# A macaron layer on one core: the second mixture of experts starts one attention step earlier

## The chip, the cores and the metric

The kernel runs on 1 core of one Trainium2 chip. The metric is the device time of one execution in microseconds (us); of several executions the median counts. TensorE multiplies matrices into the eight PSUM banks, VectorE (DVE), ScalarE (ACT) and GpSimd (POOL) do the rest, SyncE (SP) issues transfers. Each engine works through its own row of instructions in order and waits on semaphores for the others.

## The reference, cut to what matters

```python
x = x + 0.5 * ffn(layernorm(x), Wg, We, be)      # first MoE
x = x + attn(layernorm(x), Wq, Wk, Wv, Wo, Wf)   # attention
x = x + 0.5 * ffn(layernorm(x), Wg, We, be)      # second MoE
```

x is 16 sequences x 256 tokens x 128. `ffn` takes the softmax of x @ Wg over 8 experts, keeps the best 2, weighs them to a sum of 1, and adds gate * (x @ We[e] + be[e]). `attn` has 16 heads of 8; the scores of query i and key j are q.k * scale + c_i - c_j, with c the cumulative sum of log_sigmoid(x @ Wf), causal, then softmax, times v, times Wo.

## The kernel before

All of x stays in SBUF (`x_all`, 32 tiles of 128 tokens). **The MoE** goes through 8 groups of 4 tiles; its step s has four parts (`part(i, s, q)`, q = 0 to 3) on each engine and does three things for three groups at once. For group s + 2 (flag N): statistics (VectorE, line 339), rstd and shift on POOL (lines 226 to 233, part 0), xn on ScalarE (line 275, part 1), its transposes on TensorE (line 458, part 3), and their split in two parts (ScalarE line 267, VectorE line 391, part 3). For group s + 1 (flag A): twelve small matmuls to the logits (lines 447 to 449, part 1), then the gate chain on VectorE (lines 357 to 401, parts 1 to 3). For group s (flag B): per part one tile, with six matmuls of 512 columns into a low and a high bank (lines 416 and 417), four weighted sums of the low half on VectorE (line 294), four scalings of the high half on ScalarE (line 251), their sums on POOL (`add_upper`, lines 217 and 221); in part 0 also the transposed gates (lines 434, 264) and the bias (lines 441, 344). So steps -2 and -1 only prepare, and steps 0 to 7 use the experts.

**Attention** is a pipeline over sequences. Its step i has six parts: the scores of sequence i without transposition and their row maxima (lines 881 to 889; VectorE line 794), a split of the maxima on POOL (`split_max`, lines 684, 686, parts 2 and 5), their transposes (line 930) and a transfer into an extra row of q; for sequence i - 1 the turned scores (line 901), exponentials (ScalarE line 733), a causal mask per part (POOL line 673) and the product with v (line 916); for sequence i - 2 the end of it: transposes, normalisation (lines 822, 824), output projection (lines 991, 997), addition to x (line 871). The projections run two sequences ahead. Step 14 is full but for projections; step 15 has the last scores; step 16 has only turned scores (sequence 15) and the end of sequence 14; step 17 only the end of sequence 15.

The order is written out by hand in `run_layers`: `beside` takes a string in which each "a" is the next part of an attention step and each "m" the next part of an MoE step, and every engine follows that string in its own row.

The eight banks are shared. Attention uses banks 0 and 1 for scores, 2 and 3 for turned scores, 4 and 5 for the output, 6 for small things, 7 for projections (`proj_bank`, the q/k bank). The second MoE takes banks 1 and 3 as low, 2 and 4 as high, 0 for logits and transposed gates, 7 for transposes and bias. Its first tile waits until the attention's banks are free (`attn_done`, `wt_exp`).

Of the kernel before, what the change touches and what calls it, by code (L numbers as in the profile page):

```python
# [4 lines left out]
FP32 = mybir.dt.float32  # L5
# [4 lines left out]
ACT = mybir.ActivationFunctionType  # L10
AX = mybir.AxisListType

P = 128
# [4 lines left out]
def at_least(eng, sem, value):  # L18

    if isinstance(value, int) and value <= 0:  # L20
        return
    eng.wait_ge(sem, value)
# [8 lines left out]
def run_steps(eng, step, first, last, body, unroll, after=None):  # L31

    lo, hi = body
    for i in range(first, lo):
        step(i, i)
        if after is not None:
            after(i)
    with eng.Fori(0, (hi - lo) // unroll) as k:  # L40
        for part in range(unroll):
            step(k * unroll + (lo + part), lo + part)
    for i in range(hi, last):
        step(i, i)


def run_layers(eng, moe1, attention, moe2, groups, seqs, after=None):


    def moe_steps(part, first, last, after=None):  # L50
        run_steps(eng, lambda i, s: [part(i, s, k) for k in range(4)], first, last, (2, groups - 2), 2, after)

    def beside(order, i_attention, moe, i_moe):

        for at, which in enumerate(order):
            done = order[:at].count(which)
            if which == "a":
                attention(i_attention, i_attention, done)
            else:
                moe(i_moe, i_moe, done)  # L60

    moe_steps(moe1, -2, groups - 2, after)
    beside("amamammaaa", -2, moe1, groups - 2)
    beside("amamammaaa", -1, moe1, groups - 1)
    run_steps(eng, lambda i, s: [attention(i, s, k) for k in range(6)], 0, seqs - 1, (2, 2 + (seqs - 5) // 3 * 3), 3)
    beside("amaamamaam", seqs - 1, moe2, -2)
    beside("amaamamaam", seqs, moe2, -1)
    beside("aaaamamamm", seqs + 1, moe2, 0)
    moe_steps(moe2, 1, groups)


# [94 lines left out]
def moe_layer(nc, ctx, c, made, tiles, banks, x_all, tag, x_dram=None, out_dram=None, before=None):  # L166
# [5 lines left out]
    E, Q, G = c["E"], 4, x_all.shape[1] // 4  # L172
# [6 lines left out]
    y_low = [banks[0], banks[2]]  # L179
    y_high = [banks[1], banks[3]]  # L180
    gate_bank = banks[4]
    gates_t_view = gate_bank[0:3 * Q * E, P:2 * P]
    xt_bank = bias_bank = banks[5]
    logits = gate_bank[:, 0:Q * E].rearrange("p (q e) -> p q e", e=E)

    x_in = sem("x_in")
    stat_done, mom_done, eps_done = sem("stat_done"), sem("mom_done"), sem("eps_done")
# [1 line left out]
    xt_ready, hi_ready, lo_ready = sem("xt_ready"), sem("hi_ready"), sem("lo_ready")  # L189
    logits_ready, chain = sem("logits_ready"), sem("gate_chain")  # L190
    no_ready, egap_ready = sem("no_ready"), sem("egap_ready")
# [53 lines left out]
    def scalar(act):  # L245
        def experts(i, s, q):
            t = i * Q + q
            act.wait_ge(y_ready, t + 1)
            at_least(act, pair_done, t - 1)
            for j in range(4):  # L250
                last = nc.scalar.activation(scaled[:, q % 2, j], y_high[q % 2][:, j * D:(j + 1) * D], ACT.Copy,  # L251
                                            scale=gates[:, s % 2, q, 4 + j:5 + j])
            last.then_inc(high_used, 1)

        def exp_gap(i):
            act.wait_ge(chain, (i + 1) * CH + 2)
            nc.scalar.activation(egap[:, :], gap[:, :], ACT.Exp).then_inc(egap_ready, 1)

        def part(i, s, q):
            b, n = s % 2, i + 3  # L260
            N, A, B = s + 2 < G, -1 <= s and s + 1 < G, 0 <= s
            if q == 0 and B:
                act.wait_ge(gates_t_ready, i + 1)
                nc.scalar.activation(gates_t[:, :], gates_t_view, ACT.Copy).then_inc(gates_t_copied, 1)
            if q == 3 and N:
                act.wait_ge(xt_ready, n)
                nc.scalar.activation(xt_hi[:, b], xt_bank[:, :], ACT.Copy).then_inc(hi_ready, 1)
            if B:
                experts(i, s, q)
            if q == 1 and A and s >= 0:  # L270
                exp_gap(i)
            if q == 1 and N:
                act.wait_ge(shift_done, n)
                for k in range(Q):
                    last = nc.scalar.activation(xn[:, k], x_all[:, bass.ds((i + 2) * Q + k, 1), :].rearrange("p a d -> p (a d)"),  # L275
                                                ACT.Identity, scale=rstd[:, b, k:k + 1], bias=shift[:, b, k:k + 1])
                last.then_inc(xn_done, 1)
            if q == 1 and A and s < 0:
                exp_gap(i)
        return part  # L280

    def vector(dve):
# [39 lines left out]
        def part(i, s, q):  # L322
            N, A, B = s + 2 < G, -1 <= s and s + 1 < G, 0 <= s
            a, b, m, n = (s + 1) % 2, s % 2, i + 3, i + 2
            flat = gates[:, a].rearrange("p q e -> p (q e)")
            early = x_dram is not None and s < 0

            if early and s == -2 and q == 0:
# [78 lines left out]
    def tensor(pe):  # L407
        def experts(i, s, q):
            t = i * Q + q
            b = s % 2  # L410
            at_least(pe, low_chain, (t - 1) * 4)
            at_least(pe, high_used, t - 1)
            hi, lo = xt_hi[:, b, q * P:(q + 1) * P], xt_lo[:, b, q * P:(q + 1) * P]
            H = 4 * D
            for k, (x_part, w_part) in enumerate(((hi, c["we_hi"]), (hi, c["we_lo"]), (lo, c["we_hi"]))):
                nc.tensor.matmul(y_low[q % 2][:, :], x_part, w_part[:, 0:H], start=k == 0, stop=k == 2)  # L416
                last = nc.tensor.matmul(y_high[q % 2][:, :], x_part, w_part[:, H:2 * H], start=k == 0, stop=k == 2)  # L417
            last.then_inc(y_ready, 1)

        def part(i, s, q):  # L420
            a, n = (s + 1) % 2, i + 2
            N, A, B = s + 2 < G, -1 <= s and s + 1 < G, 0 <= s
            if s == -1 and q == 0 and x_dram is not None:
                pe.wait_ge(made["weights_split"], 1)
            if s == -2 and q == 3 and x_dram is not None:
                pe.wait_ge(made["filled"], 2)
            if s == 0 and q == 0 and x_dram is None:
                pe.wait_ge(before["attn_done"], 4 * G - 1)
                pe.wait_ge(before["wt_exp"], 2 * G * 12)
            if B:  # L430
                experts(i, s, q)
            if q == 0 and B:
                pe.wait_ge(gates_ready, i + 1)
                nc.tensor.transpose(gates_t_view, gates3[:, :, :].rearrange("p k n -> p (k n)").bitcast(FP32),
                                    c["ident"][:, :]).then_inc(gates_t_ready, 1)
                pe.wait_ge(gates_t_copied, i + 1)
                if A:
                    pe.wait_ge(lo_ready, n)
                if s == 0 and x_dram is not None:
                    pe.wait_ge(made["bias_hi"], 2)  # L440
                nc.tensor.matmul(bias_bank[:, :], gates_t[:, :], c["bias_split"][:, :],
                                 start=True, stop=True).then_inc(bias_ready, 1)
            if q == 1 and A:
                pe.wait_ge(lo_ready, n)
                for k in range(Q):
                    hi, lo = xt_hi[:, a, k * P:(k + 1) * P], xt_lo[:, a, k * P:(k + 1) * P]
                    nc.tensor.matmul(logits[:, k], hi, c["wg_hi"][:, :], start=True, stop=False)
                    nc.tensor.matmul(logits[:, k], hi, c["wg_lo"][:, :], start=False, stop=False)
                    last = nc.tensor.matmul(logits[:, k], lo, c["wg_hi"][:, :], start=False, stop=True)
                last.then_inc(logits_ready, 1)  # L450
            if q == 3 and N:
                pe.wait_ge(xn_done, i + 3)
                if B:
                    pe.wait_ge(bias_added, i + 1)
                else:
                    at_least(pe, lo_ready, n)
                for k in range(Q):
                    last = nc.tensor.transpose(xt_bank[:, k * P:(k + 1) * P], xn[:, k], c["ident"][:, :])
                last.then_inc(xt_ready, 1)
        return part  # L460
# [5 lines left out]
def attention_layer(nc, ctx, c, made, banks, x_all, S_LEN, before):  # L466
# [407 lines left out]
    def tensor(pe):  # L874
# [58 lines left out]
        def part(i, s, j):  # L933
# [75 lines left out]
            if j == f_part(s) + 1 and F:  # L1009
# [5 lines left out]
    return dict(constant_rows=constant_rows, sync=sync, set_up_rows=set_up_rows, zero_rows=zero_rows, set_up_zero=set_up_zero, set_up_dense=set_up_dense,  # L1015
                set_up_columns=set_up_columns, set_up_masks=set_up_masks,
                order_columns=order_columns, gpsimd=gpsimd, scalar=scalar, vector=vector, tensor=tensor,
                x_done=proj_added, attn_done=attn_done, wt_exp=wt_exp)


def program(nc, x, Wq, Wk, Wv, Wo, Wf, Wg, We, be, out):
    B, N, D = x.shape
    H, E = Wf.shape[1], Wg.shape[1]
# [3 lines left out]
    with ExitStack() as ctx:  # L1027
# [17 lines left out]
        tiles = moe_tiles(nc, ctx, E, Q, D)  # L1045
        moe1 = moe_layer(nc, ctx, c, made, tiles, banks, x_all, "m1_", x_dram=x_rows)
        attention = attention_layer(nc, ctx, c, made, banks, x_all, N, before=moe1)
        moe2 = moe_layer(nc, ctx, c, made, tiles, banks[1:5] + [banks[0], banks[7]], x_all, "m2_",
                         out_dram=out_rows, before=attention)
        block = ctx.enter_context(nc.Block())  # L1050

# [70 lines left out]
```

## Time and profile before

| what | value |
|---|---|
| three runs | 469.98, 466.66, 469.72 us; median 469.72 |
| profiled execution | 468.03 us, of which 465.9 us span (first to last instruction) |
| busy share of the span | TensorE 87%, VectorE 78%, ScalarE 60%, POOL 54% |
| mean granted TensorE clock | 0.978 of full |
| row maximum, line 794 | 192 times, mean 685 ns |
| exponential, line 733 | 192 times, mean 591 ns |
| DMA | 84 GB/s mean; nearly none from step 15 on |

The profiled execution is one run; the 2.1 us beside its span are launch and end. A stage is a stretch of the span that I cut at the first matmul of an attention step. Busy time is not needed time: what matters in a stage is which wait ends last. A wait in the trace names the instruction that waited, and behind the arrow the one that released it.

### The profile page before, as it was taken

What the parts mean: (1) busy time and instruction counts of PE and PEld (TensorE: products, weight loads), DVE (VectorE), ACT (ScalarE), POOL (GpSimd) and SP (SyncE); (2) the same over time, 40 slices, a digit from 0 to 9 for tenths busy, and PEclk for the clock granted to TensorE, in tenths of its full rate; (3) what the DMA queues carried; (4) which work ended last, traced back from release to release, by engine and by line L of the source; (5) the groups of instructions that cost most, each with busy time, mean ns of one, the idle gap of its engine ahead of it and who ended that gap; (6) DMA issues with size and microseconds to landing.
All of it is one profiled execution on the core that took longest, in us unless ns stands there. A gap on an engine that the chain in (4) does not pass through costs nothing.

```text
span 465.9 us, 11688 instructions
## 1 busy us (share of the span) xinstructions
PE 404.1 (87%) x3280; PEld 287.6 (62%) x3296; DVE 362.4 (78%) x1284; ACT 278.5 (60%) x758; POOL 249.7 (54%) x431
## 2 busy tenths in 40 slices
PE   0778888775799999999999999999998898888884
PEld 0656666553466666666667666766765676666652
DVE  3989999986877786686677678677666458999995
ACT  4666777352275566657566566655656567667753
POOL 8976666543245544544554454454445435676654
PEclk9999999887999999999999999999999899999998
DMA  3311000035644354344535535443540000001001
GB/s 112 92 56 22 0 1 0 1 100 148 171 118 152 117 155 116 111 139 111 149 102 147 134 102 149 113 147 108 152 130 9 6 1 1 25 24 45 23 23 45
DMA packets 45792, 39.11 MB, mean 84 GB/s; under 512 B 5896, under 2 KB 42524, under 8 KB 45754
## 3 DMA queue, kind: packets, MB, share of 16 engines
q1 hardware_dynamic: 43706, 38.14, 29.0%
q10 hardware_dynamic: 2048, 0.53, 0.6%
q8 instruction: 17, 0.28, 0.3%
q14 instruction: 21, 0.17, 0.1%
HBM read 22.61 MB, written 15.20 MB: 81 GB/s over the span
## 4 chain that ended last, share of the span: by engine, by line
PE 43%; POOL 22%; issue 14%; ACT 8%; DVE 5%; DMA 2%; ACTq 2%; SPq 2%; POOLq 1%; DVEq 0%
PE bank L916 10%; POOL m_pair L217 9%; PE bank L901 8%; PE bank L886 6%; ACT a_weights L733 5%; POOL m_upper L221 4%; PE bank L889 4%; PE bank L881 4%; POOL m_rstd L229 3%; PE bank L997 2%; PE bank L1008 2%; ACTq L725 2%; PE bank L1011 2%; DVE a_neg_max L794 1%; DMA x_all<-in_L_attn_x 1%
## 5 line engine op out<-in xcount | busy, mean ns | idle before, releaser
L794 DVE TENSOR_REDUCE a_neg_max<-bank 128x2 f32<-128x512 f32 (+1 forms) x192 | 123.7, 685 | 62.6 <-PE bank L889 59.9
L673 POOL TENSOR_SCALAR_AFFINE_SELECT a_weights<-a_weights 128x512 f32<-128x512 f32 (+1 forms) x96 | 75.5, 787 | 108.7 <-ACT a_weights L733 104.0
L733 ACT ACTIVATE a_weights<-bank 128x512 f32<-128x512 f32 x192 | 107.0, 591 | 35.0 <-issue 22.0
L251 ACT ACTIVATE m_scaled<-bank,m_gates 128x128 f32<-128x128 f32 x256 | 72.3, 365 | 26.2 <-PE bank L417 26.2
L901 PE MATMUL bank<-a_q_rows,a_k_rows 106*128 106x512 f32 (+1 forms) x192 | 73.7, 451 | 4.9 <-ACT a_weights L733 4.9
L217 POOL TENSOR_TENSOR m_pair<-m_scaled 128x256 f32<-128x256 f32 x64 | 47.5, 742 | 50.8 <-ACT m_scaled L251 50.7
L294 DVE SCALAR_TENSOR_TENSOR m_lower<-bank,m_gates,m_lower 128x128 f32<-128x128 f32 x192 | 66.0, 344 | 2.3 <-issue 0.2
L886 PE MATMUL bank<-a_k_rows,a_q_rows 104*128 104x256 f32 x256 | 59.3, 335 | 0.4 <-DVE a_neg_max L794 0.4
L889 PE MATMUL bank<-a_mask,a_ident 128*128 128x256 bf16 (+1 forms) x176 | 56.2, 320 | 0.0
L916 PE MATMUL bank<-a_weights,a_v 128*32 128x128 f32 x1536 | 52.7, 279 | 0.0
L886 PEld LDWEIGHTS bank<-a_k_rows,a_q_rows 104*128 104x128 f32 x256 | 40.6, 194 | 14.5 <-DVE a_neg_max L794 10.1
L916 PEld LDWEIGHTS bank<-a_weights,a_v 128*32 128x32 f32 x1536 | 39.6, 111 | 8.9 <-issue 6.4
L416 PE MATMUL bank<-we_hi,m_xt_hi 128*128 128x512 f32 x64 | 32.1, 502 | 11.9 <-DVE m_lower L294 11.3
L901 PEld LDWEIGHTS bank<-a_q_rows,a_k_rows 106*128 106x128 f32 (+1 forms) x192 | 30.9, 193 | 13.4 <-ACT a_weights L733 11.4
L881 PE MATMUL bank<-a_k_heads,a_q_dense 104*128 104x512 f32 x64 | 31.1, 524 | 5.9 <-DMA a_k_heads<-k_stage 4.4
L720 ACT ACTIVATE a_max_t<-bank 32x128 fp32r<-32x128 f32 x32 | 8.5, 265 | 42.3 <-PE bank L930 42.3
L221 POOL TENSOR_TENSOR m_upper<-m_pair 128x128 f32<-128x128 f32 x64 | 29.6, 463 | 5.7 <-POOL m_pair L217 1.3
L889 PEld LDWEIGHTS bank<-a_mask,a_ident 128*128 128x128 bf16 x192 | 19.0, 99 | 19.4 <-issue 12.5
L275 ACT ACTIVATE m_xn<-x_all,m_shift,m_rstd 128x128 f32<-128x128 f32 (+1 forms) x64 | 26.3, 484 | 4.6 <-POOL m_shift L233 4.5
L416 PEld LDWEIGHTS bank<-we_hi,m_xt_hi 128*128 128x128 f32 x64 | 12.5, 196 | 22.6 <-DVE m_lower L294 22.1
L417 PE MATMUL bank<-we_hi,m_xt_hi 128*128 128x512 f32 x64 | 26.2, 409 | 0.0
L417 PE MATMUL bank<-we_lo,m_xt_hi 128*128 128x512 f32 x64 | 26.2, 409 | 0.0
(128 smaller groups left out, 828.5 us busy)
## 6 DMA issues: line engine op xcount, KB each, us to landing
a_k_rows<-k_stage SPq DMA_DIRECT2D x16, 416.0 KB
k_stage<-a_k_parts SPq DMA_DIRECT2D x48, 128.0 KB, 1.8
q_stage<-a_q_parts SPq DMA_DIRECT2D x48, 128.0 KB, 1.9
a_q_rows<-q_stage SPq DMA_DIRECT2D x64, 96.0 KB
a_k_heads<-k_stage SPq DMA_DIRECT2D x64, 52.0 KB
a_q_dense<-q_stage SPq DMA_DIRECT2D x16, 192.0 KB
x_all<-in_L_attn_x SPq DMA_DIRECT2D x8, 256.0 KB, 2.8
out_x<-x_all SPq DMA_DIRECT2D x8, 256.0 KB, 2.3
```

Source lines behind the costliest of these rows:

```text
L217: nc.gpsimd.tensor_tensor(pair[:, q % 2], scaled[:, q % 2, 0:2], scaled[:, q % 2, 2:4], ALU.add).then_inc(pair_done, 1)
L251: last = nc.scalar.activation(scaled[:, q % 2, j], y_high[q % 2][:, j * D:(j + 1) * D], ACT.Copy, scale=gates[:, s % 2, q, 4 + j:5 + j])
L294: nc.vector.scalar_tensor_tensor(out=lower[:, q % 2, j], in0=y_low[q % 2][:, j * D:(j + 1) * D], scalar=gates[:, s % 2, q, j:j + 1], in1=t ...
L417: last = nc.tensor.matmul(y_high[q % 2][:, :], x_part, w_part[:, H:2 * H], start=k == 0, stop=k == 2)
L673: nc.gpsimd.affine_select(out=diagonal, in_=diagonal, compare_op=ALU.is_ge, fill=0.0, base=0, pattern=[[0, heads.stop - heads.start], [1, P]],
L733: nc.scalar.activation(weights[n // 2][:, half:half + 4, :].rearrange("p h n -> p (h n)"), wt_bank[n % 2][:, :], ACT.Exp).then_inc(wt_exp, 1)
L794: nc.vector.tensor_reduce(neg_max[:, t, heads], score_bank[p % 2][:, :].rearrange("p (h n) -> p h n", n=(t + 1) * P), AX.X, ALU.max, negat ...
L881: nc.tensor.matmul(bank[:, :], q_dense[:, p, :], k_heads[:, p:H:NU, :], start=True, stop=False, skip_group_check=True)
L886: nc.tensor.matmul(bank[:, n * keys:(n + 1) * keys], q_rows[b][0:KR, h, P:N], k_rows[b][0:KR, h % NU, :], start=n == 0, stop=False, skip_g ...
L889: nc.tensor.matmul(own, ident16[:, :], mask16[:, 0:heads, :], start=False, stop=True, skip_group_check=True).then_inc(scores_ready, 1)
L901: nc.tensor.matmul(bank[:, :], k_rows[b][0:rows, u, jt * P:(jt + 1) * P], q_rows[b][0:rows, u:H:NU, t * P:(t + 1) * P], start=True, stop=T ...
L916: last = nc.tensor.matmul(out_bank[t][32 * g:32 * (g + 1), u // 2 * P:(u // 2 + 1) * P], v_sb[b][:, jt * H // 2 + 2 * g + u // 2, u % 2:u ...
```

## The change

The MoE steps -2 and -1 of the second MoE move from attention steps 15 and 16 to 14 and 15. Of step 0, part 0 (tile 0) moves into step 16, behind the fifth attention part; parts 1 to 3 stay in step 17. The second MoE's banks become 0 and 2 low, 1 and 3 high, 4 for logits and gates. Since bank 4 is still the attention's in step 15 and 16, the logits and transposed gates of group 0 go to bank 7; that adds the waits for `no_ready` and `lo_ready`. Tile 0 uses banks 0 and 1 and waits for the last row maximum (`max_done`) alone; the two old waits move to tile 1.

```diff
-    run_steps(eng, lambda i, s: [attention(i, s, k) for k in range(6)], 0, seqs - 1, (2, 2 + (seqs - 5) // 3 * 3), 3)
-    beside("amaamamaam", seqs - 1, moe2, -2)
-    beside("amaamamaam", seqs, moe2, -1)
-    beside("aaaamamamm", seqs + 1, moe2, 0)
+    run_steps(eng, lambda i, s: [attention(i, s, k) for k in range(6)], 0, seqs - 2, (2, 2 + (seqs - 5) // 3 * 3), 3)
+    beside("amaamamaam", seqs - 2, moe2, -2)
+    beside("amaamamaam", seqs - 1, moe2, -1)
+    beside("aaaaama", seqs, moe2, 0)
+    beside("aaamamama", seqs + 1, moe2, 0, 1)
...
-    gates_t_view = gate_bank[0:3 * Q * E, P:2 * P]
-    logits = gate_bank[:, 0:Q * E].rearrange("p (q e) -> p q e", e=E)
+    bank_ahead = lambda g: xt_bank if g == 0 and x_dram is None else gate_bank
+    gates_t_view = lambda g: bank_ahead(g)[0:3 * Q * E, P:2 * P]
+    logits_view = lambda g: bank_ahead(g)[:, 0:Q * E].rearrange("p (q e) -> p q e", e=E)
...
             if s == 0 and q == 0 and x_dram is None:
+                pe.wait_ge(before["max_done"], 2 * G * 12)
+            if s == 0 and q == 1 and x_dram is None:
                 pe.wait_ge(before["attn_done"], 4 * G - 1)
                 pe.wait_ge(before["wt_exp"], 2 * G * 12)
...
                 pe.wait_ge(gates_ready, i + 1)
-                nc.tensor.transpose(gates_t_view, gates3[:, :, :].rearrange("p k n -> p (k n)").bitcast(FP32),
+                if s == 0 and x_dram is None:
+                    pe.wait_ge(lo_ready, n)
+                nc.tensor.transpose(gates_t_view(s), gates3[:, :, :].rearrange("p k n -> p (k n)").bitcast(FP32),
...
                     at_least(pe, lo_ready, n)
+                    if s == -1 and x_dram is None:
+                        pe.wait_ge(no_ready, n)
...
-        moe2 = moe_layer(nc, ctx, c, made, tiles, banks[1:5] + [banks[0], banks[7]], x_all, "m2_",
+        moe2 = moe_layer(nc, ctx, c, made, tiles, banks[0:5] + [banks[7]], x_all, "m2_",
```

The added lines shift the numbers: in the changed kernel line 673 is 683, 217 is 219, 221 is 223, 226 to 233 are 228 to 235, 901 is 911, 916 is 926, 416 and 417 are 419 and 420, 794 is 804, 391 is 394.

POOL's row in step 16 and at the head of step 17, before; each AFFINE_SELECT is a causal mask of sequence 15, and the last of them stands at the end of the x4:

```order
L673 AFFINE_SELECT a_weights<-a_weights 128x1024
L226 TENSOR_SCALAR m_var_eps<-m_moments 128x4
L227 TENSOR_SCALAR m_neg_mean<-m_moments 128x4
L229 TENSOR_TENSOR m_rstd<-m_var_eps,minus_half 128x4
L233 TENSOR_TENSOR m_shift<-m_neg_mean,m_rstd 128x4
L673 AFFINE_SELECT a_weights<-a_weights 128x1024
L673 AFFINE_SELECT a_weights<-a_weights 128x512 x4
L217 TENSOR_TENSOR m_pair<-m_scaled 128x256
L221 TENSOR_TENSOR m_upper<-m_pair 128x128
```

The same place in the changed kernel:

```order
L683 AFFINE_SELECT a_weights<-a_weights 128x1024 x2
L683 AFFINE_SELECT a_weights<-a_weights 128x512 x3
L219 TENSOR_TENSOR m_pair<-m_scaled 128x256
L223 TENSOR_TENSOR m_upper<-m_pair 128x128
L228 TENSOR_SCALAR m_var_eps<-m_moments 128x4
L229 TENSOR_SCALAR m_neg_mean<-m_moments 128x4
L231 TENSOR_TENSOR m_rstd<-m_var_eps,minus_half 128x4
L235 TENSOR_TENSOR m_shift<-m_neg_mean,m_rstd 128x4
L683 AFFINE_SELECT a_weights<-a_weights 128x512
```

The rstd group left the head of the step, and the last mask now stands behind the upper sum of tile 0 and the rstd group of group 2.

TensorE's row at the end of step 16 and the head of step 17, before; turned scores 8 to 11 are the two x2 of line 901, and line 916 the products with v:

```order
L901 MATMUL bank<-a_q_rows,a_k_rows 128x512 x2
L991 MATMUL bank<-ident,a_attn 128x128 x2
L901 MATMUL bank<-a_q_rows,a_k_rows 128x512 x2
L925 MATMUL bank<-ident,a_out_t 128x128 x2
L997 MATMUL bank<-wo,a_attn_t 128x128 x2
L916 MATMUL bank<-a_weights,a_v 32x128 x16
L458 MATMUL bank<-ident,m_xn 128x128 x4
L916 MATMUL bank<-a_weights,a_v 32x128 x16
L925 MATMUL bank<-ident,a_out_t 128x128 x2
L416 MATMUL bank<-we_hi,m_xt_hi 128x512
```

In the changed kernel, from tile 0 to the products with v:

```order
L419 MATMUL bank<-we_hi,m_xt_hi 128x512
L420 MATMUL bank<-we_hi,m_xt_hi 128x512
L419 MATMUL bank<-we_lo,m_xt_hi 128x512
L420 MATMUL bank<-we_lo,m_xt_hi 128x512
L419 MATMUL bank<-we_hi,m_xt_lo 128x512
L420 MATMUL bank<-we_hi,m_xt_lo 128x512
L442 MATMUL bank<-ident,m_gates 96x128
L449 MATMUL bank<-bias_split,m_gates_t 128x512
L911 MATMUL bank<-a_q_rows,a_k_rows 128x512 x2
L935 MATMUL bank<-ident,a_out_t 128x128 x2
L1007 MATMUL bank<-wo,a_attn_t 128x128 x2
L926 MATMUL bank<-a_weights,a_v 32x128 x32
```

Tile 0 with its gates and bias moved ahead of turned scores 10 and 11; the transposes of line 458 are gone from here, so that the products with v of steps 16 and 17 stand in one piece.

VectorE's row in step 15, before; each TENSOR_REDUCE is a row maximum:

```order
L794 TENSOR_REDUCE a_neg_max<-bank 128x4 x2
L339 BN_STATS m_stats<-x_all 128x6 x4
L348 BN_AGGR m_moments<-m_stats 128x2 x4
L794 TENSOR_REDUCE a_neg_max<-bank 128x4 x2
L794 TENSOR_REDUCE a_neg_max<-bank 128x2 x4
L822 RECIPROCAL a_recip<-bank 128x16
```

And in the changed kernel:

```order
L394 TENSOR_TENSOR m_xt_lo<-bank,m_xt_hi 128x512
L804 TENSOR_REDUCE a_neg_max<-bank 128x4 x2
L342 BN_STATS m_stats<-x_all 128x6 x4
L351 BN_AGGR m_moments<-m_stats 128x2 x4
L804 TENSOR_REDUCE a_neg_max<-bank 128x4 x2
L804 TENSOR_REDUCE a_neg_max<-bank 128x2 x2
L360 MAX m_best<-bank 128x8 x4
L380 TENSOR_TENSOR m_gap<-m_best 128x4
L382 MAX_INDEX m_best_no<-m_best,bank 128x8 x4
L804 TENSOR_REDUCE a_neg_max<-bank 128x2 x2
```

The low part of the transposes stands ahead of the first row maximum of the step, and the first piece of the gate chain between the sixth and the seventh.

## Rows read from the trace of the kernel before

**Rows 1.** Busy time by stage: stretch, its length, then busy us (instructions) of each engine, PEclk, DMA

```profile
337.65:351.67 14.02, 14.02 (x160) 9.94 (x157) 9.49 (x19) 8.41 (x18) 7.06 (x13) 1.00 0.43 116
351.67:366.63 14.96, 13.77 (x156) 9.45 (x153) 10.18 (x25) 9.33 (x21) 7.16 (x15) 1.00 0.02 4
366.63:381.18 14.55, 12.94 (x143) 9.03 (x139) 6.16 (x35) 9.47 (x22) 6.43 (x11) 0.88 0.01 3
381.18:395.54 14.36, 12.77 (x91) 9.42 (x90) 11.46 (x55) 8.89 (x30) 6.22 (x12) 1.00 0.00 1
```

**Rows 2.** Who waited for whom, step 15: total us, times, longest

```profile
PE bank L930 <- POOL a_max_parts L686: 0.8, 1, 0.8
```

**Rows 3.** Timeline of POOL: start, us, line, operation [idle before <-releaser]

```profile
343.82 0.22 POOL L686 TENSOR_TENSOR a_max_parts<-a_neg_max,a_max_parts 128x16 fp32r<-128x16 f32 x1
...
377.31 0.63 POOL L673 TENSOR_SCALAR_AFFINE_SELECT a_weights<-a_weights 128x512 f32<-128x512 f32 x1 [2.23 <-ACT a_weights L733]
...
386.12 0.74 POOL L217 TENSOR_TENSOR m_pair<-m_scaled 128x256 f32<-128x256 f32 x1 [5.45 <-ACT m_scaled L251]
...
386.94 0.46 POOL L221 TENSOR_TENSOR m_upper<-m_pair 128x128 f32<-128x128 f32 x1
...
389.18 0.20 POOL L233 TENSOR_TENSOR m_shift<-m_neg_mean,m_rstd 128x4 f32<-128x4 f32 x1
```

**Rows 4.** Timeline of TensorE, steps 14 to 17

```profile
345.06 0.27 PE L930 MATMUL bank<-ident,a_max_parts 128*32 128x128 f32 x1
...
353.29 0.40 PE L881 MATMUL bank<-a_k_heads,a_q_dense 104*128 104x512 f32 x1
...
366.63 0.66 PE L458 MATMUL bank<-ident,m_xn 128*128 128x128 f32 x4
...
370.51 1.94 PE L916 MATMUL bank<-a_weights,a_v 128*32 128x128 f32 x32
...
373.39 0.21 PE L447 MATMUL bank<-wg_hi,m_xt_hi 128*128 128x8 f32 x1
...
374.74 0.72 PE L901 MATMUL bank<-a_q_rows,a_k_rows 106*128 106x512 f32 x2
...
377.90 0.99 PE L901 MATMUL bank<-a_q_rows,a_k_rows 106*128 106x512 f32 x2
...
381.18 1.08 PE L916 MATMUL bank<-a_weights,a_v 128*32 128x128 f32 x32
...
382.96 0.48 PE L416 MATMUL bank<-we_hi,m_xt_hi 128*128 128x512 f32 x1
...
385.07 0.51 PE L441 MATMUL bank<-bias_split,m_gates_t 96*128 96x512 f32 x1 [0.36 <-ACT m_gates_t L264]
```

**Rows 5.** Timeline of ScalarE, steps 16 and 17

```profile
373.20 1.09 ACT L733 ACTIVATE a_weights<-bank 128x512 f32<-128x512 f32 x2 [1.99 <-PE bank L901]
...
374.44 1.65 ACT L275 ACTIVATE m_xn<-x_all,m_shift,m_rstd 128x128 f32<-128x128 f32 x4
...
384.92 1.12 ACT L251 ACTIVATE m_scaled<-bank,m_gates 128x128 f32<-128x128 f32 x4
```

**Rows 6.** Timeline of VectorE, steps 16, 17 and after

```profile
367.95 0.69 DVE L391 TENSOR_TENSOR m_xt_lo<-bank,m_xt_hi 128x512 fp32r<-128x512 f32 x1 [1.76 <-ACT m_xt_hi L267]
...
377.33 0.69 DVE L401 TENSOR_TENSOR m_hot<-m_hot,m_g 128x64 f32<-128x64 f32 x1
...
383.24 0.26 DVE L822 RECIPROCAL a_recip<-bank 128x16 f32<-128x16 f32 x1 [0.63 <-PE bank L925]
...
388.58 0.39 DVE L357 MAX8 m_best<-bank 128x8 f32<-128x8 f32 x4 [0.34 <-PE bank L449]
...
402.90 0.21 DVE L401 TENSOR_TENSOR m_hot<-m_hot,m_g 128x64 f32<-128x64 f32 x1
```

**Rows 7.** Busy time and granted clock of two stretches at the start of step 16

```profile
368.00:370.00 2.00, 0.56 (x2) 0.24 (x2) 1.80 (x9) 1.25 (x4) 0.00 (x0) 1.00 0.03 7
370.00:372.00 2.00, 2.00 (x29) 1.52 (x33) 0.00 (x0) 0.97 (x2) 1.78 (x4) 0.54 0.01 1
```

More of the change, by code:

```diff
@@ L51, in moe_steps, with beside @@
         run_steps(eng, lambda i, s: [part(i, s, k) for k in range(4)], first, last, (2, groups - 2), 2, after)
-    def beside(order, i_attention, moe, i_moe):
+    def beside(order, i_attention, moe, i_moe, first=0):
         for at, which in enumerate(order):
@@ L59, in beside @@
             else:
-                moe(i_moe, i_moe, done)
+                moe(i_moe, i_moe, first + done)
     moe_steps(moe1, -2, groups - 2, after)
@@ L263, in part @@
                 act.wait_ge(gates_t_ready, i + 1)
-                nc.scalar.activation(gates_t[:, :], gates_t_view, ACT.Copy).then_inc(gates_t_copied, 1)
+                nc.scalar.activation(gates_t[:, :], gates_t_view(s), ACT.Copy).then_inc(gates_t_copied, 1)
             if q == 3 and N:
@@ L325, in part @@
             flat = gates[:, a].rearrange("p q e -> p (q e)")
+            logits = logits_view(s + 1)
             early = x_dram is not None and s < 0
@@ L422, in part @@
             N, A, B = s + 2 < G, -1 <= s and s + 1 < G, 0 <= s
+            logits = logits_view(s + 1)
             if s == -1 and q == 0 and x_dram is not None:
@@ L1017, in attention_layer @@
                 order_columns=order_columns, gpsimd=gpsimd, scalar=scalar, vector=vector, tensor=tensor,
-                x_done=proj_added, attn_done=attn_done, wt_exp=wt_exp)
+                x_done=proj_added, attn_done=attn_done, wt_exp=wt_exp, max_done=max_done)
 def program(nc, x, Wq, Wk, Wv, Wo, Wf, Wg, We, be, out):
```

## The prediction

> **What bounds the kernel now.** I read first the busy time by stage [rows 1]. I call the 18 attention steps 0 to 17, as the code counts them. Step 14 is a full step (scores of sequence 14, turned scores of 13, projection of 12) with nothing of the second MoE beside it: TensorE is busy for all of its 14.02 us, VectorE for 9.49. Step 15 carries the first quarter-turn of the second MoE (its step -2) and takes 14.96 us, of which TensorE works 13.77. Step 16 has no scores any more, only turned ones, and MoE step -1 beside it: 14.55 us, with VectorE busy 6.16 and a mean granted clock of 0.88. Step 17 carries all four tiles of group 0: 14.36 us, VectorE 11.46. From 395.54 us on there is only MoE, in code that the change leaves as it is. So the change is worth what it does to the 57.89 us of these four stages; all their work stays, and only idle time can go or come. TensorE's idle time in them is 0 + 1.19 + 1.61 + 1.59 = 4.39 us, and some 1.4 us more lie in the slower clock of step 16. That, about 5.8 us, is the most that the change can gain.
>
> Next I read the waits of step 15 [rows 2]: TensorE stands once, for 0.8 us, at the transpose of the row maxima, because POOL splits them late, behind the four small operations of rstd. Then the timelines, one engine after the other [rows 3 to 6]. At the start of step 16 TensorE waits for exponentials: it does 0.56 us of work in 2 us, and in the next 2 us its granted clock is 0.54, so that it runs mostly at 1.2 GHz instead of 2.4 [rows 7]. The 32 matmuls of line 916 take 1.94 us there and 1.08 us in step 17 [rows 4].
>
> **Step 14 gets MoE step -2.** TensorE gains the four transposes of xn (0.6 us; they start at 366.63 and the next work at about 367.2 [rows 4]). They can't hide, since TensorE has no idle time here. POOL gains the rstd group ahead of its second causal mask. In step 17 that group runs from 387.40, where the upper sum ends, to 389.38: 2.0 us [rows 3]. In step 14 POOL finishes the first maxima at 344.04 without it [rows 3], and TensorE takes them at 345.06 [rows 4]. With it POOL ends at 346.05, so TensorE waits 1.0 us, much as the 0.8 us in step 15 shows [rows 2]. VectorE's statistics (1.3 us) fit in its 4.5 us of idle time, ScalarE's xn (1.65 us [rows 5]) in its 5.6. Step 14: +1.6 us. Bounds: +0.6 if POOL's group is hidden, +2.5 if ScalarE's xn adds another 0.9 to an exponential.
>
> **Step 15 gets step -1 in place of -2.** Statistics, rstd, xn and transposes it has already. New are: (a) xt_lo of group 0 at its head, which VectorE must do before the first row maximum. xt_lo ends 368.64 - 366.63 = 2.01 us after the transposes began [rows 4, 6]; a row maximum takes 0.69, so the first score bank comes free at 2.70. TensorE wants it 0.6 for the transposes + 1.62 (353.29 [rows 4] - 351.67 [rows 1]) = 2.22 us after that beginning. Cost 0.5, and 0.1 at the second bank. (b) The twelve logit matmuls, 374.74 - 373.39 = 1.35 us [rows 4]. They stand before the fourth part of the step, thus before the transpose that waited 0.8 us for POOL [rows 2], and take up that wait: cost 0.6. (c) VectorE's gate chain, some 3 us in three pieces: its work goes from 10.18 to about 13.2 + 0.7 = 13.9 us of a stage that grows to 16. The first piece (maxima, gap, indices, 1.2 us) runs while TensorE does two score groups, a transpose, two turned scores and line 916, some 3.5 us, against 1.2 + 2 x 0.69 = 2.6 us on VectorE. I cost it at nothing; if none of it were hidden it is the rival below. Step 15: +1.2 us (bounds 0.6 and 4.2).
>
> A row on the gate chain speaks against me: the product on line 401 took 0.69 us at 377.33, beside POOL's mask of 0.63 us from 377.31, and 0.21 us at 402.90 with POOL idle [rows 3, 6]. The Trainium skill, "SBUF — State Buffer", section "Who interferes with whom", says that a VectorE instruction with two inputs in SBUF and a GpSimd instruction that reads SBUF exclude each other for its whole length. The row agrees. Four more such operations of the chain now lie beside masks; by the rule each could lose up to the 0.5 us seen, 2 us in all, still inside VectorE's idle time; without the rule it is nothing.
>
> **Step 16 loses step -1 and gets tile 0.** I count in times of before, as if its head had not moved. The first 6.8 us stay, the waits and the slow clock too, as the same exponentials stand there. From 373.4 the logits go, but they stood in a wait: turned scores 6 need exponential 4, which ends at 373.75 [rows 5] against their start at 374.74 [rows 4], so 0.95 us are won. Then ScalarE's xn (1.65 us) no longer holds the exponentials back: line 916 ends at about 375.9, turned scores 8 and 9 and the transposes of the output at 376.65. Tile 0, the transposed gates and the bias take what they took in step 17, 382.96 to 385.42 = 2.45 us [rows 4]: 379.1. From turned scores 10 at 377.90 to 381.18 were 3.28 us [rows 4], less 0.6 for the transposes and 0.5 for a wait of these scores: 2.2. So step 17 begins at 381.3, where it began before, with tile 0 done.
>
> But the last causal mask is late. On POOL it now stands behind pair, upper sum and rstd of group 2. ScalarE scales tile 0 from 378.55 to 379.7 (1.12 us [rows 5]), pair and upper end 1.28 us later at 381.0, rstd (2.0) at 383.0, the mask (0.63) at 383.7 [rows 3]. TensorE has done the first half of line 916 at 381.8, waits 1.9 us, and ends the second at 384.2 (before: 382.26). Behind it in TensorE's row stand tile 1 and all of step 17.
>
> **Step 17 has three tiles.** Tile 1 takes 1.45 us (384.2 to 385.7), the logits 1.35: VectorE can start on them at 387.1, before at 388.58 [rows 6]: -1.5 us. Both kernels then have the same VectorE work, except that the normalisation of sequence 15 (two operations, the first 0.26 us [rows 6]; I take 0.5) now comes after that point and not before it. Steps 16 and 17: -1.0 us. The new waits cost nothing by themselves: lo_ready and no_ready are long past, max_done comes before step 16, and the attention waits of tile 1 are over at 382.5.
>
> **Sum.** +1.6 + 1.2 - 1.0 = +1.8 us. The profiled execution took 468.03 us (span 465.9, 2.1 around it), so it would be 469.8; on the median of 469.72 that is 471.5 us.
>
> **Rivals.** *The clock falls again* (0.22). A wait of 1.9 us is longer than the two of 0.7 and 0.8 that went ahead of the slow stretch of step 16. If it has the same effect, line 916, tile 1 and part of the logits run at 1.2 GHz: as much as before, 1.4 to 1.7 us. 471.5 + 1.6 = 473.1. Against it: TensorE was fully busy ahead of this wait.
>
> *VectorE becomes the bound of the full steps* (0.09). TensorE has two score banks and stands when VectorE is late with a maximum. If nothing of the added VectorE work hides, step 14 costs 1.9 and step 15 3.7 us (13.9 - 10.2) beside its 0.6 of TensorE: +6.2 - 1.0 = +5.2, 474.9 us, slower by 1.1%. It decides if the gaps of VectorE before its maxima in step 15 are gone. Against it: 4.5 us of idle time in step 14, and step 15 took 1.3 us of statistics without such a wait.
>
> *The mask is not late* (0.17). If POOL's queue runs ahead in step 14 and 17 (TensorE reaches both points later than I count), 1.0 and 1.9 us fall away: -1.1 us, 468.6. For it: the 0.8 us of rows 2 was all that POOL's order cost in step 15.
>
> *Most idle time goes* (0.04). The slow clock of step 16 stays away as well, and the waits at its head: near the most of 5.8 us; 464.5.
>
> My forecast has 0.48. The range of 8 in 10 goes from 467.5 to 475.2: the ends are the mask rival less 1 us and the VectorE rival. A difference of 1%, 4.7 us, is about what a measurement of this kernel can tell from none: faster by more 0.04, within it 0.86, slower by more 0.10.
>
> **What would show it.** Right: in the changed profile step 14 takes about 15.6 us and step 15 about 16.1; TensorE waits about 1 us at the transpose of the maxima in step 14 and no more in step 15; POOL's last causal mask comes 3 us after its last exponential and TensorE waits nearly 2 us for it; MoE step 1 begins about 1.8 us later than 395.54. Wrong: VectorE's maxima back to back through step 15 (second rival), a PEclk digit below full in step 17 (first), no wait of TensorE on POOL (third), or a step of the pure MoE tail that differs from before.

## The result, and the profile after

| | median | lowest | highest | executions |
|---|---|---|---|---|
| before | 466.75 us | 465.03 | 471.73 | 20 |
| changed | 470.18 us | 468.41 | 474.34 | 20 |

The ratio is 1.007 (95% interval 1.0046 to 1.0095): the change costs 3.3 us (2.1 to 4.4). The median of before is 3 us lower than the 469.72 us of the first three executions, from which the forecast was counted. The forecast was +1.8 us, with a rival of +3.4 us (the clock falls again). Ratios and means below leave out two executions in a slower state: one of the kernel before (471.27 us, clock 0.973) and one of g2_prep (627.13 us, clock 0.564).

The profiled execution of the changed kernel took 473.95 us, near the top of its range; its mean granted clock was 0.967. These are its busy times by stage, for step 14, step 15, and steps 16 and 17 together (from the transposes of line 468 to the first statistics of MoE step 1); columns as in [rows 1], where the last stage is 366.63 to 395.54:

```profile
337.33:352.72 15.39, 14.60 (x164) 10.41 (x161) 10.53 (x27) 9.72 (x22) 8.71 (x17) 1.00 0.42 105
352.72:368.96 16.24, 14.78 (x168) 10.82 (x166) 13.55 (x47) 10.04 (x23) 7.08 (x14) 1.00 0.02 4
368.96:399.02 30.06, 24.35 (x218) 17.55 (x215) 13.48 (x60) 16.58 (x47) 11.25 (x19) 0.89 0.01 2
```

Step 14 grew from 14.02 to 15.39 us, step 15 from 14.96 to 16.24, and the rest from 28.91 to 30.06. VectorE is busy for 13.55 us of step 15, as worked out (13.9); TensorE has 0.8 us of idle time in step 14, where it had none, and 1.5 in step 15.

TensorE's timeline of the same profile, at its waits. They stand where the forecast put them: 0.79 us for the split maxima in step 14 (line 940), 0.50 for the first row maximum of step 15 (line 891), 1.94 for the last causal mask (line 926). One of 0.96 us was priced at nothing (line 896, a row maximum behind the second piece of the gate chain). The transpose of the maxima in step 15, which waited 0.8 us before [rows 2], waits no more.

```profile
345.69 0.27 PE L940 MATMUL bank<-ident,a_max_parts 128*32 128x128 f32 x1 [0.79 <-POOL a_max_parts L696]
...
354.98 0.50 PE L891 MATMUL bank<-a_k_heads,a_q_dense 104*128 104x512 f32 x1 [0.50 <-DVE a_neg_max L804]
...
365.66 0.50 PE L896 MATMUL bank<-a_k_rows,a_q_rows 104*128 104x256 f32 x2 [0.96 <-DVE a_neg_max L804]
...
372.70 1.83 PE L926 MATMUL bank<-a_weights,a_v 128*32 128x128 f32 x32
...
377.58 1.94 PE L926 MATMUL bank<-a_weights,a_v 128*32 128x128 f32 x32
...
387.39 0.65 PE L926 MATMUL bank<-a_weights,a_v 128*32 128x128 f32 x16 [1.94 <-POOL a_weights L683]
```

And POOL at that last mask: pair and rstd of the MoE stand ahead of it, and TensorE goes on at 387.39, just after it ends at 387.25; the forecast's chain, link for link.

```profile
383.41 0.72 POOL L219 TENSOR_TENSOR m_pair<-m_scaled 128x256 f32<-128x256 f32 x1 [1.45 <-ACT m_scaled L253]
...
384.76 0.24 POOL L228 TENSOR_SCALAR m_var_eps<-m_moments 128x4 f32<-128x4 f32 x1
...
386.46 0.20 POOL L235 TENSOR_TENSOR m_shift<-m_neg_mean,m_rstd 128x4 f32<-128x4 f32 x1
...
386.61 0.64 POOL L683 TENSOR_SCALAR_AFFINE_SELECT a_weights<-a_weights 128x512 f32<-128x512 f32 x1
```

The second loss of this execution is the clock. After its head, step 16 ran slowly for about 7 us and not for 3.4 as in [rows 4, 7] (lines 926 at 1.83 and 1.94 us), and the clock fell once more in the plain MoE steps, from 403.6 to some 410. Two windows of the changed kernel; PEclk is the third number from the right:

```profile
375.00:378.00 3.00, 2.74 (x14) 1.37 (x16) 0.28 (x2) 2.45 (x5) 0.63 (x1) 0.50 0.02 5
405.00:408.00 3.00, 3.00 (x8) 2.31 (x9) 1.76 (x11) 1.35 (x5) 1.23 (x2) 0.50 0.00 0
```

So one profile against one profile says +6.0 us of span where the ratio says +3.3. A pair of executions that differ in their clock can't price a change; I needed more profiles.

### The profile page after: what moved, and what is told of

The parts are those of the page before. It is cut to its first block, busy times and chain, and to the rows that moved or that the text cites. A ratio compares the mean times of both kernels' runs of the same rounds, so it can differ in the third digit from the quotient of the medians.

```text
span 471.9 us, 11705 instructions
## 1 busy us (share of the span) xinstructions
PE 406.0 (86%) x3296; PEld 290.0 (61%) x3296; DVE 362.4 (77%) x1284; ACT 278.9 (59%) x758; POOL 249.4 (53%) x431
## 4 chain that ended last, share of the span: by engine, by line
PE 41%; POOL 19%; issue 13%; ACT 8%; DVE 8%; DMA 4%; SPq 4%; ACTq 2%; POOLq 1%; DVEq 0%
PE bank L926 9%; POOL m_pair L219 8%; PE bank L911 7%; PE bank L896 6%; ACT a_weights L743 5%; PE bank L899 4%; POOL m_upper L223 4%; PE bank L891 3%; POOL m_rstd L231 3%; PE bank L1007 2%; PE bank L1018 2%; PE bank L1021 2%; DVE m_lower L296 2%; ACTq L735 2%; DMA a_k_heads<-k_stage 1%
## 5 line engine op out<-in xcount | busy, mean ns | idle before, releaser
L899 PE MATMUL bank<-a_mask,a_ident 128*128 128x256 bf16 (+1 forms) x192 | 62.7, 327 | 0.0
L911 PEld LDWEIGHTS bank<-a_q_rows,a_k_rows 106*128 106x128 f32 (+1 forms) x192 | 31.3, 195 | 13.5 <-ACT a_weights L743 10.9
L296 DVE SCALAR_TENSOR_TENSOR m_lower<-bank,m_gates,x_all 128x128 f32<-128x128 f32 x64 | 21.7, 340 | 6.9 <-PE bank L420 6.1
```

What stands on the lines that cost most here:

```text
L296: nc.vector.scalar_tensor_tensor(out=lower[:, q % 2, j], in0=y_low[q % 2][:, j * D:(j + 1) * D], scalar=gates[:, s % 2, q, j:j + 1], in1=t ...
L899: nc.tensor.matmul(own, ident16[:, :], mask16[:, 0:heads, :], start=False, stop=True, skip_group_check=True).then_inc(scores_ready, 1)
L911: nc.tensor.matmul(bank[:, :], k_rows[b][0:rows, u, jt * P:(jt + 1) * P], q_rows[b][0:rows, u:H:NU, t * P:(t + 1) * P], start=True, stop=T ...
```

## The experiments

Each ratio is against the kernel before on the same chip. The runs e1 to e4 were on one chip, those with f and g on another, on which the changed kernel itself was not run.

| run | what | ratio | 95% interval |
|---|---|---|---|
| e4_same | changed kernel again | 1.0088 | 1.0054 to 1.0121 |
| e1_prep_only | no tile in step 16 | 1.0018 | 0.9985 to 1.005 |
| e2_mask_first / g3_mask | last mask first on POOL | 1.0029 / 0.9996 | 0.9999 to 1.0059 / 0.9964 to 1.0027 |
| e3_filled | waits filled with matmuls | 1.0069 | 1.0041 to 1.0096 |
| f2_dve | mask first, VectorE's order | 0.9994 | 0.9962 to 1.0027 |
| f3_all / g1_all | and POOL's, ScalarE's in step 14 | 0.9967 / 0.9945 | 0.9938 to 0.9996 / 0.9914 to 0.9976 |
| f4_prep_all / g2_prep | all orders, no tile in step 16 | 0.9984 / 0.9974 | 0.9952 to 1.0016 / 0.9943 to 1.0005 |

### Both kernels again

> The changed kernel once more, as a control on the same chip: ratio 1.005 to 1.0095 again. Its profile shows another execution: where the clock falls (step 16 for 3.4 or 6.8 us, and once in the MoE tail) differs from the first profile if that is chance; the waits of 0.8 us (step 14), 0.5 and 0.96 us (step 15) and 1.94 us (step 17) stand in it unchanged.

> The kernel before once more, for a second profile. Theory A: stages of 14.0 and 15.0 us for steps 14 and 15 again; step 16 and 17 together take 28.9 us if TensorE's clock falls in step 16 as in the first profile, and about 27.4 us if it doesn't, so that the change costs nothing or 0.2 us there instead of winning 1. Rival: steps 16 and 17 take 28.9 us with or without a fall of the clock.

In both new profiles the clock stays full through all four stages. Busy time by stage, the kernel before (466.19 us):

```profile
337.20:351.21 14.01, 14.01 (x160) 9.95 (x156) 9.50 (x19) 8.42 (x18) 7.05 (x13) 1.00 0.44 116
351.21:366.18 14.97, 13.78 (x156) 9.40 (x152) 10.11 (x25) 9.33 (x21) 7.04 (x15) 1.00 0.02 4
366.18:393.83 27.65, 24.19 (x233) 17.43 (x229) 17.25 (x89) 18.40 (x52) 12.67 (x23) 1.00 0.01 2
```

and the changed kernel:

```profile
337.02:352.42 15.40, 14.60 (x164) 10.37 (x161) 10.53 (x27) 9.73 (x22) 8.75 (x17) 1.00 0.41 105
352.42:368.67 16.25, 14.99 (x167) 10.81 (x165) 13.54 (x47) 10.04 (x23) 7.09 (x14) 1.00 0.02 4
368.67:396.30 27.63, 21.73 (x218) 15.74 (x215) 13.51 (x61) 16.48 (x47) 11.28 (x19) 1.00 0.01 2
```

Step 14 costs 1.39 us, step 15 1.28, steps 16 and 17 nothing (27.65 against 27.63): 2.65 us together. Without the fall of the clock the stage of before is 27.65 us and not 28.91, so the first profile held 1.3 us of slow clock there: theory A of f1_before (27.4) holds, its rival doesn't. The waits stand in the changed kernel's new profile too, with 0.80, 0.51 and 1.95 us; that of 0.96 was 0.75.

Turned scores 6 and 7 of step 16, which in the change lose the logits ahead of them, without a fall of the clock; first the kernel before, then the changed one:

```profile
372.78 0.71 PE L901 MATMUL bank<-a_q_rows,a_k_rows 106*128 106x512 f32 x2
```

```profile
374.62 0.98 PE L911 MATMUL bank<-a_q_rows,a_k_rows 106*128 106x512 f32 x2 [0.45 <-ACT a_weights L743]
```

They start 6.60 us after the stage's transposes before, and 5.95 after: 0.65 us are won here.

Part of the wait of 0.75 to 0.96 us in step 15 is the interference that the prediction had noted and taken to be hidden in VectorE's idle time. In the changed kernel's first profile, POOL's mask and the second piece of the gate chain ran side by side just before the maximum that TensorE wanted:

```profile
364.10 0.64 POOL L683 TENSOR_SCALAR_AFFINE_SELECT a_weights<-a_weights 128x512 f32<-128x512 f32 x1 [2.58 <-ACT a_weights L743]
```

```profile
364.24 0.50 DVE L399 TENSOR_TENSOR m_g<-m_egap,m_g 128x4 f32<-128x4 f32 x1
...
364.92 2.69 DVE L804 TENSOR_REDUCE a_neg_max<-bank 128x2 f32<-128x512 f32 x4
```

The mask and the product of line 399 both end at 364.74. In e4_same that product started ahead of the mask and took 0.16 us, and the next one (line 404) 0.59 instead of 0.22. So one of the two lost some 0.35 us in either profile.

The times agree. Every execution reports its mean granted clock. Of 90 executions of before (all those taken beside the runs of this section) 43 had 0.984 or more, mean 466.21 us; of 30 of the changed kernel 10, mean 468.91: +2.70 us (give or take 0.5) for the placement. Over all, the means are 467.37 and 470.53, +3.2 (give or take 0.8). The other 0.5 us is smaller than these uncertainties. It fits the clock: if a clock below 1 is taken as time at half speed, the changed kernel has 19.1 us of it per execution, before 16.8. That the change causes this isn't shown.

The end of step 17 shows a loss that I had priced too low. VectorE of the kernel before, from the logits (line 357) to the next step:

```profile
386.86 0.39 DVE L357 MAX8 m_best<-bank 128x8 f32<-128x8 f32 x4 [0.34 <-PE bank L449]
...
390.42 0.15 DVE L396 TENSOR_TENSOR m_g<-m_egap,m_g 128x4 f32<-128x4 f32 x1
...
390.75 0.50 DVE L401 TENSOR_TENSOR m_hot<-m_hot,m_g 128x64 f32<-128x64 f32 x1
...
393.10 0.55 DVE L303 TENSOR_TENSOR x_all<-m_lower,m_upper 128x128 f32<-128x128 f32 x1
...
393.83 0.86 DVE L339 BATCH_NORM_STATS2 m_stats<-x_all 128x6 f32<-128x128 f32 x4
```

and of the changed kernel (line 360 is 357 before, 399 is 396, 404 is 401, 305 is 303, 832 and 834 are 822 and 824):

```profile
388.26 0.39 DVE L360 MAX8 m_best<-bank 128x8 f32<-128x8 f32 x4 [0.99 <-PE bank L457]
...
390.17 0.24 DVE L832 RECIPROCAL a_recip<-bank 128x16 f32<-128x16 f32 x1
...
390.45 0.29 DVE L834 TENSOR_TENSOR a_attn<-bank,a_recip 128x128 f32<-128x128 f32 x1
...
391.96 0.70 DVE L399 TENSOR_TENSOR m_g<-m_egap,m_g 128x4 f32<-128x4 f32 x1
...
392.85 0.41 DVE L404 TENSOR_TENSOR m_hot<-m_hot,m_g 128x64 f32<-128x64 f32 x1
...
395.11 0.67 DVE L305 TENSOR_TENSOR x_all<-m_lower,m_upper 128x128 f32<-128x128 f32 x1
...
396.30 0.86 DVE L342 BATCH_NORM_STATS2 m_stats<-x_all 128x6 f32<-128x128 f32 x4
```

From the first of these rows to the last it takes 6.97 us before and 8.04 after. The normalisation at 390.17 is 0.5 of the difference, as forecast. Another 0.55 is the small product of line 399, 0.70 us where it was 0.15. POOL's pair sum ran just then:

```profile
391.84 0.80 POOL L219 TENSOR_TENSOR m_pair<-m_scaled 128x256 f32<-128x256 f32 x1 [2.42 <-ACT m_scaled L253]
```

It ends at 392.64 and the product at 392.66. That is the rule of the Trainium skill, "SBUF — State Buffer", section "Who interferes with whom": a VectorE instruction with two inputs in SBUF and a GpSimd instruction reading SBUF shut each other out. The measured 0.55 us agrees with it, and here VectorE had no idle time to hide it in. It isn't chance: this product took 0.69 or 0.70 us in the eight profiles with tile 0 in step 16 and 0.15 or 0.16 in the five without. No run moved the pair sum alone, so that the port is the cause rests on the page and on the two ends.

### No tile in step 16

```diff
-    beside("aaaaama", seqs, moe2, 0)
-    beside("aaamamama", seqs + 1, moe2, 0, 1)
+    beside("aaaaaa", seqs, moe2, 0)
+    beside("aaaamamamm", seqs + 1, moe2, 0)
```

> Only the two preparing MoE steps move to attention steps 14 and 15 (banks as in the changed kernel); step 16 has no MoE part, step 17 all four tiles. Theory A (costs by place: +2.6 us in steps 14 and 15, and the late last causal mask, 1.9 us, comes from tile 0 in step 16): steps 14 and 15 take 15.4 and 16.2 us as in the changed kernel, TensorE waits for no mask at the head of step 17, step 16 is about 2.4 us shorter than with tile 0, and the time is 0 to 1 us above the kernel before (ratio 1.000 to 1.002). Rival B (the slow clock does it: with the logits gone from step 16 TensorE idles more there, its clock stays low longer): the clock in step 16 is low for about 7 us instead of 3.4 in most profiles, and the time is as bad as the changed kernel's, ratio 1.005 or more.

TensorE has no wait for a mask at the head of step 17 here. Ratio 1.0018; steps 14 and 15 take 15.39 and 16.24 us as in the changed kernel. Steps 16 and 17, the clock full:

```profile
368.94:395.13 26.19, 22.34 (x217) 15.63 (x213) 13.05 (x60) 16.17 (x46) 11.03 (x19) 1.00 0.01 2
```

26.19 us against 27.63 with tile 0 in step 16. So as built, the tile in step 16, which has only turned scores, loses 1.4 us. Theory A's ratio and its steps 14 and 15 came out. Step 16 is 1.5 us shorter than with the tile and not 2.4, from the transposes to the products with v at its end (10.97 against 12.49). The clock rival is not borne out: with the logits gone from step 16 here as well, this profile shows no slow stretch there. But that is one profile, and the upper end of the interval is the rival's 1.005.

### The last mask first

The diff is cut: each engine also hands its name to `run_layers` as `who`.

```diff
-    beside("aaaaama", seqs, moe2, 0)
+    beside("aaaaaam" if who == "POOL" else "aaaaama", seqs, moe2, 0)
```

> The changed kernel with one change on POOL: in step 16 its MoE part comes behind the last causal mask. Theory A: TensorE's wait of 1.94 us for that mask goes, and nothing else is late, so 1.5 to 1.9 us less than the changed kernel, ratio to the kernel before 1.003. Rival B (clock): the ratio stays within 0.001 of the changed kernel's 1.007, as another part of step 17 waits instead or the clock eats it.

> e2_mask_first once more, to halve the uncertainty of what the late mask cost. Theory A: 2.2 us (27.63 - 25.44 between two undisturbed profiles) of the changed kernel's 3.3, ratio 1.002 to 1.004. Rival (the profile's 2.2 us come back elsewhere): 1.005 or more.

TensorE does all 64 matmuls with v in one piece, without a wait, and the stage takes 25.44 us:

```profile
380.26 1.96 PE L926 MATMUL bank<-a_weights,a_v 128*32 128x128 f32 x64
```

```profile
367.77:393.21 25.44, 21.50 (x218) 15.71 (x215) 13.47 (x60) 16.46 (x47) 11.28 (x19) 1.00 0.01 2
```

2.19 us less than with the mask behind the MoE part; g3_mask's profile has 25.43 us there. The ratios of the two runs, 1.0029 and 0.9996, lie about 2 and 3.5 us below the changed kernel's 1.007: more than half of the loss was this one place in POOL's queue. 0.9996 is lower than the 1.002 to 1.004 expected, though its interval reaches 1.0027. Tile 0 in step 16 then wins 0.75 us against e1 (25.44 against 26.19).

### Matmuls in the waits of step 16

```diff
+            if s == NSEQ - 1 and n in (2, 3):
+                if n == 2:
+                    pe.wait_ge(max_done, NSEQ * 12)
+                for _ in range(3):
+                    nc.tensor.matmul(score_bank[0][:, :], ident16[:, :], mask16[:, :, :], start=True, stop=True)
```

> The changed kernel with six matmuls of 512 columns into an unused score bank, in two lots of three, where TensorE waits for exponentials at the head of step 16 (they compute nothing that is used). Theory A (placement alone): each lot takes some 0.65 us inside a wait of 0.75 to 0.84, so the time stays, ratio 1.007. Rival B (clock): TensorE's clock no longer falls in step 16, 1.4 to 3.4 us less, ratio 1.001 to 1.004, and the granted clock of steps 16 and 17 is 1.00.

The waits of 0.74 and 0.84 us shrink to nothing and 0.18, at no cost (line 911 is now the added matmuls, 916 the turned scores; they start as long after the transposes as in e4_same, 1.97 and 3.31 us):

```profile
370.02 0.82 PE L911 MATMUL bank<-a_mask,a_ident 128*128 128x512 bf16 x3
...
370.93 0.50 PE L916 MATMUL bank<-a_q_rows,a_k_rows 109*128 109x512 f32 x1
...
371.27 0.82 PE L911 MATMUL bank<-a_mask,a_ident 128*128 128x512 bf16 x3
...
372.27 0.50 PE L916 MATMUL bank<-a_q_rows,a_k_rows 109*128 109x512 f32 x1 [0.18 <-ACT a_weights L743]
```

but the ratio is 1.0069, as without them. The clock stays full in step 16 of this profile and then falls at about 386, a microsecond after the wait of 1.95 us for the mask, for 10 us (0.58 is the mean of 12 us):

```profile
371.00:384.00 13.00, 10.97 (x143) 7.26 (x143) 4.38 (x18) 7.92 (x19) 6.78 (x11) 1.00 0.02 4
384.00:396.00 12.00, 11.08 (x50) 9.14 (x51) 5.15 (x30) 4.69 (x15) 3.01 (x6) 0.58 0.00 0
```

So these waits aren't what decides about the clock, or not alone. Of the twelve profiles in which they are not filled, five have a fall in step 16 (both first profiles, f2_dve, g1_all, g2_prep) and seven have none. Nor did the filling change the clock over all executions: the mean is 0.9795 in the twelve of e3_filled and in the ten of e4_same. Rival B's lower ratio did not come.

### The orders of steps 14 and 15 mended

VectorE first, on top of the mask (cut: the other engines keep their strings, and `a_first` is the first attention part):

```diff
+    if who == "DVE":
+        beside("amaamamaa", seqs - 2, moe2, -2)
+        beside("a", seqs - 1, moe2, -1)
+        moe2(-2, -2, 3)
+        beside("maamaamam", seqs - 1, moe2, -1, a_first=1)
```

> The changed kernel with POOL's mask first (as before) and VectorE's order mended in two places: the low part of the transposes comes behind the first two row maxima of step 15, and the second piece of the gate chain behind the maxima of its fifth part. Theory A: TensorE's waits of 0.50 and 0.96 us for row maxima in step 15 go, 1.0 to 1.5 us less than with the mask first alone, ratio 1.000. Rival (VectorE bounds step 15): the waits only move behind the next maxima, and the ratio stays at 1.002 to 1.003.

```profile
335.95:351.32 15.37, 14.58 (x165) 10.43 (x161) 10.53 (x27) 9.72 (x22) 8.72 (x17) 1.00 0.38 105
351.32:366.30 14.98, 14.59 (x167) 10.83 (x166) 12.54 (x43) 10.03 (x23) 6.22 (x12) 1.00 0.02 4
```

Step 15 takes 14.98 us instead of 16.25, and no wait for a row maximum is left in it: the 0.50 and 0.75 to 0.96 us are gone. The gate chain and twelve logit matmuls now lie in it at no cost against the kernel before. The ratio, 0.9994, is theory A's, but it can't confirm the gain: on the same chip the mask alone had 0.9996, so the 1.3 us rest on the profiles. Then POOL and ScalarE in step 14:

```diff
+        beside({"POOL": "aaammaamam", "ACT": "amaaaammam"}.get(who, "amaamamaam"), seqs - 2, moe2, -2)
```

> As f2_dve, and in step 14 POOL's rstd group comes behind the split of the first maxima, ScalarE's xn behind the exponentials of the fifth part. Theory A: TensorE's wait of 0.8 us in step 14 goes too, ratio 0.998, 1 us below the kernel before. Rival: ScalarE is late with the exponentials at the head of step 15 instead, ratio 1.000 or more.

> f3_all once more. If its orders mend what the change cost (theory A), the ratio is 0.994 to 1.000 again and its profile has steps 14 and 15 of 14.45 and 14.98 us and 25.4 us from the transposes of step 16 to the first statistics of MoE step 1, where the clock doesn't fall. Rival (the first 12 executions were lucky with the clock): ratio 1.001 or more.

```profile
336.72:351.17 14.45, 14.45 (x165) 10.37 (x161) 10.53 (x27) 9.55 (x22) 8.17 (x16) 1.00 0.42 112
351.17:366.15 14.98, 14.58 (x168) 10.80 (x165) 12.53 (x43) 10.30 (x24) 6.87 (x13) 1.00 0.02 4
366.15:391.58 25.43, 21.67 (x218) 15.75 (x215) 14.35 (x65) 16.47 (x47) 12.06 (x21) 1.00 0.01 2
```

Step 14 falls from 15.37 to 14.45 us, TensorE busy throughout: what is left of its cost is the transposes. The four stages take 54.86 us, against 56.63 before and 59.28 as changed. The ratios 0.9967 and 0.9945 lie below 1 with their whole intervals: this version beats both kernels by its order alone, 465.8 and 465.4 us. The clock fell in step 16 of g1_all's profile, and the last stage took 27.92 us there.

> All orders of f3_all for steps 14 and 15, but no tile in step 16 (all four in step 17). Theory A: as f3_all less what tile 0 gives in step 16; from the profiles of the first four runs I expect both within 0.5 us of each other, ratio 0.998. Rival (the tile in step 16 is what pays): 1 to 2 us above f3_all.

> f4_prep_all once more (all orders mended, no tile in step 16). Theory A, from the profiles: 0.75 us slower than g1_all in an execution without a fall of the clock there (26.2 against 25.4 us), so ratio 0.998 to 0.999. Rival (the tile in step 16 is worth nothing once the clock is counted): at or below g1_all.

Without the tile in step 16, steps 16 and 17 take 26.18 us again, 0.75 more than with it:

```profile
365.52:391.70 26.18, 22.63 (x217) 15.65 (x213) 13.94 (x64) 16.14 (x46) 11.82 (x21) 1.00 0.01 2
```

The ratios, 0.9984 and 0.9974, lie between 1 and those of f3_all and g1_all. The differences to them, 0.8 and 1.4 us, are within the intervals, so the tile's gain rests on the profiles, and on undisturbed ones: where the clock fell in step 16, g1_all has 27.92 us with the tile and g2_prep 28.14 without.

## Why the prediction was right or wrong

- **Direction, range and the places of three waits: right.** 470.18 us lies in 467.5 to 475.2, slower by 0.7%, inside the 1% that got 0.86. That the time came within 1.3 us of the 471.5 forecast is luck: the three executions that I counted from were 3 us too slow, and the change cost 1.5 us more than the sum.
- **Step 14: right.** +1.6 forecast, +1.39 measured (wait 0.79, not 1.0); f3_all took the wait away with POOL's order.
- **Step 15: sum right (+1.2, +1.28), parts not quite.** (a) 0.50, as forecast. (b) The logits took up POOL's wait, as forecast. (c) The gate chain was priced at nothing, from its first piece alone. Its second piece stood right before a maximum that TensorE wanted: 0.75 to 0.96 us, of which some 0.35 is the interference with POOL's mask. That the sum came out is partly luck: before, step 15 also had a wait of 0.4 us for an exponential that went.
- **Steps 16 and 17: the step that failed.** -1.0 forecast, 0.0 measured between undisturbed profiles. The late mask was right to 0.05 us (1.9; 1.94 and 1.95). From the transposes to VectorE's start on the logits behind tile 1 the gain was 20.68 - 19.59 = 1.1 us (f1_before, e4_same), not 1.5: I had read it off a head of step 16 with the slow clock, as if that belonged to the kernel. Turned scores 6 start 8.11 us after the transposes in the first profile, but 6.60 in f1_before and 5.95 in e4_same, so the logits' place was worth 0.65 us and not 0.95; the remaining 0.1 is not traced. Behind it +1.07, not +0.5: the product of line 399 beside POOL's pair sum, the kind of loss that the prediction had noted beside POOL's masks and taken to be hidden.
- **What the stages leave open.** They explain +2.65 of the 3.3 us; the rest lies inside the uncertainty of the ratio.
- **The clock rival: partly.** Of three profiles with the late mask (the changed kernel twice, e3_filled) the clock fell at that wait in one, e3_filled. In the mean the clock accounts for at most the 0.5 us above, not 1.6, as far as the executions tell: a fall comes in some of them only, and before has such stretches too. In the changed kernel's first profile it fell elsewhere, in its second nowhere in these stages.
- **VectorE as the bound of full steps: half a truth.** TensorE did wait for maxima in step 15, 1.25 to 1.46 us. But VectorE as a whole didn't bound it (13.5 of 16.2 us busy); only the place of two pieces in its row did, and f2_dve moved them.

## What to carry to other kernels

In this kernel, work put beside a full stage was paid by where it stood in each engine's queue, not by the engine's idle time: the same work cost 2.65 us in one order and won 1.8 us in another, by undisturbed stages of the profiles. When one string orders all engines, ask for each engine apart what stands behind the new piece, and put what another engine waits for (a mask, a row maximum) ahead of it. And take a second profile of the kernel before: one execution's slow clock looks like the kernel's own.

## What the hardware showed that I had not expected

The same program's granted clock falls at different places from one execution to the next: in step 16 (first profile of before, for 3.4 us; those of the changed kernel, f2_dve, g1_all and g2_prep, for about 7), nowhere in the four stages (f1_before, e4_same), or between 395 and 404 us in the plain MoE steps, where TensorE had been busy for 2.4 to 2.5 of the 3 us ahead. A fall of 7 us in step 16 made the last stage 2.4 us longer (30.06 against 27.63) and 2.5 with all orders mended (27.92 against 25.43). In the changed kernel a mean of 0.967 went with 473.95 us and one of 0.986 with 468.41. What sets off a fall stays open; with two waits of 0.8 us filled with matmuls it came later in the one profile, and no less in the mean. It was not tried whether a longer filling at the late mask would.
